# Routing tokens to regions of their two experts in DRAM, in a graph layer with eight experts on one Trainium2 core

## The chip, the cores and the metric

The kernel runs on one core of a Trainium2 chip. The metric is the device time of one execution in microseconds (us). The engines are TensorE (PE, with its weight loads as PEld), VectorE (DVE), ScalarE (ACT), GpSimd (POOL) and SyncE (SP), which here only starts DMAs. Each runs its own list of instructions in order; they meet at semaphores.

## The reference

A graph of 3125 nodes with 256 features and 50000 edges. The layer is a layer norm, two graph convolutions and a linear attention whose results are added to the input, and then a mixture of experts on the normed tokens:

```
xn = layernorm(x)
x = x + gnn(xn, edges) + attention(xn)
tokens = layernorm(x)
probs = softmax(tokens @ router_w.T)            # 8 experts
rw, re = top_k(probs, 2);  rw = rw / rw.sum()
combine = zeros(N, 8).at[arange(N)[:, None], re].set(rw)
out = tokens
for e in range(8):
    h = gelu(tokens @ w1[e] + b1[e])            # 256 -> 256
    out = out + combine[:, e:e+1] * (h @ w2[e] + b2[e])   # 256 -> 256
x = x + out
```

Every token has a weight other than zero for exactly two of the eight experts. All is float32; the kernel makes the expert products from a high and a low float32r part (hi*hi + hi*lo + lo*hi, the table `THREE`), so three matmuls stand for one.

## The kernel before

The 3125 nodes lie in SBUF as 25 slots of 125 partitions; five slots make a chunk (`W` = 5 slots, `C` = 5 chunks, `PT` = 125). The program has these stages:

1. Loads, edge bookkeeping and the projections of the graph and attention weights (0 to 135 us of the trace).
2. The first graph convolution. DVE writes one-hot tiles (`hot_unit`, L584), PE turns 8 of them into counts (`build`, L1009), ACT copies those to SBUF (`take_counts`, L1276), and PE sums with them (`add_sum`, L1092). There are eight blocks of counts (`CH`) of 4 MB, of which three fit in SBUF, so SP stores the first five in DRAM (`kept`, L441) and loads them again (L445). A block may be built over block k only after the store of block k has landed: ACT waits for `kept_ok` (L1283).
3. The second graph convolution (sums from the kept counts, to 510 us). Then, chunk by chunk, PE merges (`merge_transposed`, L1145) and multiplies by the second weights (`times_w2`, L1161), and DVE adds to `acc`, takes mean and variance (L844 to L855) and writes the normed tokens `tok` (L867). PE transposes `tok` (L1170), ACT copies the transposes and splits off the high part (L1385, L1388), DVE the low part (L835), PE makes the router logits (L1179). Meanwhile ACT casts both expert weights to `w_hi` (L1392) and POOL subtracts to make `w_lo` (L484).
4. The router: one pass over all 25 slots on DVE (L878 to L916): top 2, softmax, weights `comb`. Then the second bias is added to `acc` through a small matmul with `comb` (L1202 to L1217, L922).
5. The experts: a hardware loop over five chunks, and inside it all eight experts on all 625 tokens of the chunk. `up` (L1225) makes 24 matmuls of 312 or 314 columns per expert and chunk, ACT applies Gelu with the bias and makes the high part of it (L1428, L1433), DVE the low part (L949), PE makes 30 matmuls of 256 columns (L1251), and DVE adds the result times the token's weight for that expert to `acc` in SBUF (`take`, L930). SP stores each chunk when it is done (L454).

What decides the order is the code of each engine as written and the semaphores; nothing schedules it.

## Time and profile before

| | us |
|---|---|
| median of 3 runs | 905.37 (905.05 to 905.47) |
| the profiled execution | 905.5 |
| its span, first to last instruction | 903.7 |
| stage 5, experts | 614.3 to 899.6 |

In the page, part 1 gives each engine's busy time, part 2 the span in 40 slices of 22.6 us, part 4 the chain of work that ended last. A stage is read from the table of stretches (busy time of each engine in a stretch that one names), and a single hand-over from the instructions in order of time. The granted clock is given as a share of full speed: 1.00 is 2.4 GHz, 0.50 is 1.2 GHz.

### The profile page before, as it was taken

Reading aid. Unit: us, or ns where it says so; the run is one execution under the profiler, and the core shown is the slowest. Engines: PE = TensorE matmul, PEld = TensorE weight load, DVE = VectorE, ACT = ScalarE, POOL = GpSimd, SP = SyncE. Lnnn points to the kernel's source line nnn. Section 1 sums busy time; section 2 is a strip of 40 time slices with the busy share of each in tenths; the row PEclk is TensorE's granted clock in tenths of the full one; section 3 lists DMA queues with packets and bytes.
Section 4 is the critical chain, followed back from the end, with each engine's and each line's share of the span. In section 5 each row is a group of like instructions: output and inputs, shape, how many; then the busy total and the mean of one; then the engine's idle time right before and its main releaser. Section 6 shows DMA issues by size and latency. Waiting matters only on the chain.

```text
span 903.7 us, 16245 instructions
## 1 busy us (share of the span) xinstructions
PE 768.5 (85%) x6482; PEld 700.6 (78%) x6482; DVE 563.4 (62%) x1146; ACT 370.7 (41%) x673; POOL 23.7 (3%) x20
## 2 busy tenths in 40 slices
PE   1697846639999999969999997459999999999997
PEld 0253425539999999749999996448999999999997
DVE  5959986689999995561111188864555455554554
ACT  0036443717777775011111232325434444444442
POOL 1000000000000000000000003300000000000000
PEclk9789786959999999979999998659999999999999
DMA  7200040004444000004862320000000000000000
GB/s 166 51 1 1 1 181 1 1 0 180 183 183 180 7 1 2 1 0 183 339 274 116 112 77 1 1 0 1 1 29 0 0 28 0 28 0 0 28 0 28
DMA packets 10381, 53.98 MB, mean 60 GB/s; under 512 B 1596, under 2 KB 7800, under 8 KB 9050
## 3 DMA queue, kind: packets, MB, share of 16 engines
q1 hardware_dynamic: 10330, 53.25, 16.0%
q8 instruction: 38, 0.62, 0.3%
q14 instruction: 13, 0.11, 0.0%
HBM read 29.57 MB, written 23.68 MB: 59 GB/s over the span
## 4 chain that ended last, share of the span: by engine, by line
PE 68%; DVE 23%; ACT 4%; DMA 2%; issue 1%; SPq 0%; DVEq 0%; POOL 0%; ACTq 0%; POOLq 0%
PE psB L1100 17%; PE psC L1251 8%; PE psD L1251 8%; PE psA L1231 8%; PE psB L1231 8%; PE psC L1100 3%; DVE hot_b L589 3%; PE psA L1017 3%; PE psC L1006 2%; DVE hot_k L589 2%; ACT counts L1285 2%; DMA acc<-in_x_dram 2%; PE psD L1017 2%; PE psD L1157 2%; DVE small L855 1%
## 5 line engine op out<-in xcount | busy, mean ns | idle before, releaser
L1100 PE MATMUL psB<-hs,counts 125*128 125x256 f16 x1600 | 211.4, 276 | 3.4 <-DVE hs L704 2.7
L1100 PEld LDWEIGHTS psB<-hs,counts 125*128 125x128 f16 x1600 | 173.2, 141 | 5.1 <-issue 2.8
L949 DVE TENSOR_TENSOR h_lo<-g_sb,h_hi 128x625 fp32r<-128x625 f32 x80 | 61.2, 807 | 110.0 <-ACT h_hi L1433 110.0
L589 DVE TENSOR_TENSOR hot_b<-iota_j,brow 128x1024 bf16<-128x1024 bf16 x128 | 88.3, 690 | 11.0 <-PE psA L1017 7.6
L1428 ACT ACTIVATE g_sb<-psA,eb 128x312 f32<-128x312 f32 x80 | 37.4, 519 | 129.8 <-PE psA L1231 128.1
L589 DVE TENSOR_TENSOR hot_k<-iota_j,key 128x1000 bf16<-128x1000 bf16 x128 | 86.1, 673 | 0.0
L1017 PE MATMUL psA<-hot_k,hot_b 128*128 128x125 bf16 x512 | 50.9, 224 | 37.0 <-DVE hot_k L589 29.8
L1285 ACT CAST counts<-psA 128x1000 f16<-128x1000 f32 x64 | 63.3, 989 | 38.3 <-PE psA L1017 38.3
L1017 PEld LDWEIGHTS psA<-hot_k,hot_b 128*128 128x128 bf16 x512 | 39.1, 99 | 47.0 <-DVE hot_k L589 35.9
L1285 ACT CAST counts<-psD 128x1000 f16<-128x1000 f32 x64 | 63.6, 993 | 14.3 <-PE psD L1017 14.3
L768 DVE TENSOR_TENSOR sum_both<-psB,sum_both 128x256 f32<-128x256 f32 x32 | 13.5, 422 | 79.7 <-ACT sum_both L1349 79.7
L936 DVE SCALAR_TENSOR_TENSOR acc<-psC,comb,acc 125x256 f32 x100 | 42.7, 476 | 18.7 <-PE psD L1251 18.7
L1006 PE MATMUL psC<-wcat,xnT 128*125 128x512 f32 x100 | 53.4, 662 | 0.8 <-ACT xnT L1270 0.8
L1433 ACT CAST h_hi<-g_sb 128x625 fp32r<-128x625 f32 x80 | 53.1, 719 | 0.0
L1100 PE MATMUL psC<-hs,counts 125*128 125x256 f16 x400 | 52.2, 273 | 0.0
L1017 PE MATMUL psD<-hot_k,hot_b 128*128 128x125 bf16 x512 | 51.0, 224 | 1.0 <-DVE hot_k L589 1.0
L936 DVE SCALAR_TENSOR_TENSOR acc<-psD,comb,acc 125x256 f32 x100 | 42.7, 477 | 13.8 <-PE psC L1251 13.8
L1428 ACT ACTIVATE g_sb<-psB,eb 128x312 f32<-128x312 f32 x80 | 37.4, 520 | 26.6 <-PE psB L1231 26.6
L1017 PEld LDWEIGHTS psD<-hot_k,hot_b 128*128 128x128 bf16 x512 | 40.7, 100 | 8.9 <-DVE hot_k L589 4.6
L1349 ACT COPY sum_both<-psB 128x256 f32<-128x256 f32 x32 | 12.0, 376 | 80.6 <-PE psB L1100 80.6
L1100 PEld LDWEIGHTS psC<-hs,counts 125*128 125x128 f16 x400 | 43.5, 140 | 0.0
L1251 PE MATMUL psC<-w_hi,h_hi 128*125 128x256 f32 x200 | 40.4, 283 | 0.0
(268 smaller groups left out, 1482.5 us busy)
## 6 DMA issues: line engine op xcount, KB each, us to landing
kept_counts<-counts SPq DMA_DIRECT2D x5, 4000.0 KB, 11.8
counts<-kept_counts SPq DMA_DIRECT2D x5, 4000.0 KB, 13.2
w_raw<-in_L_ffn_w_dram SPq DMA_DIRECT2D x2, 2048.0 KB, 12.0
acc<-in_x_dram SPq DMA_DIRECT2D x1, 2800.0 KB
out_dram<-acc SPq DMA_DIRECT2D x5, 560.0 KB
wcat<-in_L_mix_w_qkv_dram SPq DMA_DIRECT2D x1, 384.0 KB
acc<-in_x_dram SPq DMA_DIRECT2D x1, 325.0 KB
out_dram<-acc SPq DMA_DIRECT2D x5, 65.0 KB
```

Of the source, the lines that this page charges most:

```text
L589: v.tensor_tensor(hot[:, slot], iota_j[:, 0:n, :].unsqueeze(1).to_broadcast([P, pairs, n, PAIR]), val[:, cols].rearrange("p (g s) -> p g s ...
L936: y = v.scalar_tensor_tensor(a, out_place(f, d), cw, a, ALU.mult, ALU.add)
L949: v.tensor_tensor(h_lo[:, e % 2, h, :], g_sb[:, h, :], h_hi[:, e % 2, h, :].bitcast(F32), ALU.subtract).then_inc(hidden_low_ok, 1)
L1006: m = pe.matmul(psC[0:PT, 512 * (n % 2):512 * (n % 2) + 512], xnT[:, n % 2, k, :], wcat[:, k, :], start=(k == 0), stop=(k == 1))
L1017: m = pe.matmul(ps[:, bank + KEYS * q:bank + KEYS * q + KEYS], hot_b[:, slot, (GROUP * (j % 2) + q) // PAIR, :, q % PAIR], hot_k[:, slot, ...
L1100: m = pe.matmul(sum_bank(g, d), counts5[0:PT, buf, a, d, :], hs2[0:PT, a, :, :].rearrange("p q f -> p (q f)"), start=a == 0 and first, sto ...
L1157: m = pe.matmul(o, part2[:, part, k, HID * d:HID * d + HID], sel[:, k, PT * c:PT * c + PT], start=False, stop=(k == SECOND_ORDER[-1] and p ...
L1231: m = pe.matmul((psA, psB)[h][:, 512 * n:512 * n + size], (w_hi, w_lo)[a][:, 0, e, k, P * h:P * h + P], (tokT_hi, tokT_lo)[b][:, k, bass.d ...
L1251: m = pe.matmul(out_place(f, d), (h_hi, h_lo)[a][:, f % 2, k, PT * d:PT * d + PT], (w_hi, w_lo)[b][:, 1, f, k, :], start=(i == 0 and k == ...
L1285: act.copy(counts[:, k % BUFFERS, UNIT * u:UNIT * u + UNIT, :].rearrange("p (h s) j -> p h (s j)", h=2), (psA, psD)[unit % 2][:, :].rearra ...
L1428: g = act.activation(g_sb[:, h, at + had:at + size], (psA, psB)[h][:, 512 * n + had:512 * n + size], ACT.Gelu, bias=eb1[:, 2 * e + h:2 * e ...
L1433: act.copy(h_hi[:, e % 2, h, :], g_sb[:, h, :]).then_inc(hidden_high_ok, 1)
```

## The change

All eight experts on all tokens become two experts per token.

- **Regions.** A DRAM tensor `slots` has a region of 3328 rows (`REGION`) for each expert and 256 spare rows. A row is 265 floats (`ROW`, 1060 bytes): the token, its eight weights and its node number. After the inputs have landed, SP fills all of it with zeros, in pieces of 130 floats: 28.5 MB, ahead of the kept counts in SP's queue.
- **Router by chunk.** The pass of stage 4 becomes `router(c)`, in five parts between the chunks of stage 3. PE computes each token's place in its expert's region from sums of one-hot rows (`ranks`), DVE makes it an address (`slot_places`), and POOL scatters the chunk's 125-row slots: 10 indirect DMAs a chunk (5 slots, 2 experts each), 50 in all. The tiles `rows` are double-buffered; before DVE writes the tokens of chunk c it waits for the scatters of chunk c-2.
- **Output.** `x + tokens` of a chunk goes to `out` at once (SP waits for `tok_added`).
- **Tiles.** `MOE_TILES` is 32: tiles of 256 rows of one expert, the worst case; a table made by DVE (`tab_e`, `tab_r`) says for each which expert and where. For each tile SP loads the rows (`xs`, four buffers) and copies the expert's first weights from SBUF to SBUF (`w1_now`, two buffers, two copies of 2 KB per partition); PE transposes the rows (4 transposes), makes `up` (12 matmuls of 256 columns) and `down` (14, with the second bias as one of 7 for each half); ACT and DVE split and apply Gelu as before, on 512 columns; DVE multiplies by the weight into `y` (three buffers); POOL adds `y` to `out` by two indirect DMAs that accumulate. POOL waits until all adds of the tile before have landed (`added`). Rows that are all zero get node number 4095 and are left out by the bounds check. SP, ACT, DVE and PE each read the expert's number from SBUF into a register (`value_load`), SP the place too.
- **Weights' low part.** `w_lo` moves from POOL to DVE, behind the last `slot_places`.
- **One-hot tiles.** The two DVE instructions of `hot_unit` (1024 and 1000 elements) become one of 2048.

```diff
+            sp.wait_ge(zeros_ok, 1)
+            sp.wait_ge(in_x, 32)
+            for e in range(EXPERTS + 1):
+                size = REGION if e < EXPERTS else SLOT
+                run = 130 if e < EXPERTS else 106
...
             for k in range(SPILLED):
                 sp.wait_ge(counts_ok, UNITS * (k + 1))
...
+            sp.wait_ge(table_ok, 2)
+            sp.wait_ge(spread, 16 * 2 * SLOTS)
+            sp.wait_ge(w_lo_ok, 2)
+            for t in range(-2, MOE_TILES):
+                if t + 2 < MOE_TILES:
+                    n = t + 2
+                    at = sp.value_load(tab_r[0:1, n:n + 1], min_val=0, max_val=EXPERTS * REGION)
...
+                    sp.dma_start(xs[:, n % X_BUFS], slots[bass.ds(at, SLOT), :].rearrange("(p q) f -> p q f", q=2)).then_inc(slots_in[n % X_BUFS], 16)
+                if t >= 0:
+                    e = sp.value_load(tab_e[0:1, t:t + 1], min_val=0, max_val=EXPERTS - 1)
+                    if t >= 2:
+                        sp.wait_ge(upped, 2 * t - 2)
+                    for part, w in enumerate((w_hi, w_lo)):
+                        sp.dma_start(w1_now[:, t % 2, part].bitcast(F32), w[:, 0, bass.ds(e, 1), :, :].rearrange("p a k f -> p (a k) f").bitcast(F32)).then_inc(w1_now_in[t % 2], 16)
...
-                pool.tensor_tensor(w_lo[:, i], w_raw[:, i], w_hi[:, i].bitcast(F32), ALU.subtract).then_inc(w_lo_ok, 1)
...
+            for c in range(C):
+                pool.wait_ge(weights_in_row, c + 1)
+                pool.wait_ge(place_ok, c + 1)
+                for d in range(W):
+                    for j in range(2):
+                        n = W * c + d
+                        pool.indirect_dma_start(slots[:, :], bass.IndirectOffsetOnAxis(place[0:PT, j, n:n + 1], 0), rows[0:PT, c % 2, d, :],
+                                                None).then_inc(spread, 16)
+            pool.wait_ge(stored, 32 * C)
+            for t in range(MOE_TILES):
+                if t:
+                    pool.wait_ge(added, 16 * 2 * t)
+                for q in range(2):
+                    pool.wait_ge(y_ok, 2 * t + q + 1)
...
+                    pool.indirect_dma_start(out[:, :], bass.IndirectOffsetOnAxis(to_row[:, t % 3, q:q + 1], 0), y[:, t % 3, q, :], None,
+                                            bounds_check=NODES - 1, oob_is_err=False, compute_op=ALU.add).then_inc(added, 16)
...
+                if c >= 2:
+                    slot_places(c - 2)
                 v.wait_ge(std_ok, c + 3)
                 st.did(v.reciprocal(rstd[0:PT, 0:W], small[0:PT, 3, 0:W]))
                 st.wait()
...
+                if c >= 2:
+                    v.wait_ge(spread, 16 * 2 * W * (c - 1))
```

In order, the places that matter. DVE in chunk 2, before: statistics, the addition of the chunk before, then the tokens.

```order
L850 BN_STATS stats<-acc 125x6 x4
L853 BN_AGGR mv<-stats 125x2 [waits vector_done]
L853 BN_AGGR mv<-stats 125x2 x4
L855 TENSOR_SCALAR small<-mv 125x5 [waits vector_done]
L859 TENSOR_TENSOR acc<-acc,tok 125x1280 [waits tok_ok]
L861 RECIPROCAL rstd<-small 125x5 [waits std_ok]
L867 TENSOR_SCALAR tok<-acc,mv,rstd 125x256 [waits tok_transposed,tok_added,vector_done]
L867 TENSOR_SCALAR tok<-acc,mv,rstd 125x256 x4
```

The same place in the change (`rows` holds the tokens, `spread` counts landed scatters):

```order
L986 TENSOR_SCALAR small<-mv 125x5 [waits vector_done]
L958 TENSOR_TENSOR place_of<-psC,region_at 125x40 [waits rank_in]
L960 TENSOR_REDUCE members<-member 125x8
L962 TENSOR_TENSOR passed<-passed,members 125x8 [waits vector_done]
L963 TENSOR_TENSOR picked<-pick,place_of 125x80
L965 TENSOR_REDUCE place_f<-picked 125x10 [waits vector_done]
L967 CAST place<-place_f 125x2x5 [waits vector_done]
L990 RECIPROCAL rstd<-small 125x5 [waits std_ok]
L995 TENSOR_SCALAR rows<-acc,mv,rstd 125x256 [waits spread,vector_done]
L995 TENSOR_SCALAR rows<-acc,mv,rstd 125x256 x4
```

The places of chunk 0 are made here, and two instructions on DVE waits for the scatters that use them.

POOL in the change, at the last scatters and the first two tiles; before, POOL had only the two `w_lo` subtractions and a memset in this part of the program.

```order
L565 DMA expert_slots<-rows,place 26880x265 [waits place_ok,weights_in_row]
L565 DMA expert_slots<-rows,place 26880x265 x9
L574 DMA out_dram<-y,to_row 3125x256 [waits gate_row_ok,y_ok,stored]
L574 DMA out_dram<-y,to_row 3125x256 [waits gate_row_ok,y_ok]
L574 DMA out_dram<-y,to_row 3125x256 [waits gate_row_ok,y_ok,added]
L574 DMA out_dram<-y,to_row 3125x256 [waits gate_row_ok,y_ok]
```

Each tile's two adds now stand in a row, and the first of them waits for the landing of the two before.

PE in the change, `down` of one tile (`psC` and `psD` take one half each), with the read of the expert's number ahead of it; before, this was a row of 30 matmuls per expert and chunk without such a read.

```order
L1344 TENSOR_LOAD tab_e
L1344 ISA x2
L1377 ISA [waits y_ok,hidden_low_ok]
L1377 MATMUL psC<-b_both,b_ones 128x256
L1380 ISA
L1380 MATMUL psC<-w_hi,h_hi 128x256
L1380 ISA
L1380 MATMUL psC<-w_hi,h_hi 128x256
```

The two ISA lines and the load set up registers; `down` moved behind them, once for each of 32 tiles.

## Rows read from the trace of the kernel before

**Rows 1.** The page, part 1: busy time in us (share of the span), instructions
```profile
PE 768.5 (85%) x6482; PEld 700.6 (78%) x6482; DVE 563.4 (62%) x1146; ACT 370.7 (41%) x673; POOL 23.7 (3%) x20
```
**Rows 2.** Stretches: us, each engine's busy us (instructions), PEclk, DMA share, GB/s
```profile
215.00:350.00 135.00, 129.28 (x1508) 124.57 (x1507) 128.99 (x227) 103.16 (x131) 0.00 (x0) 1.00 0.29 123
...
510.00:614.00 104.00, 70.58 (x708) 65.65 (x706) 76.70 (x221) 32.73 (x50) 19.74 (x3) 0.79 0.13 41
614.00:904.00 290.00, 283.00 (x2160) 282.09 (x2160) 143.26 (x280) 123.27 (x240) 0.00 (x0) 0.99 0.04 11
```
**Rows 3.** The chain that ended last, 664 to 690 us: start, us, what
```profile
679.38 3.00 PE psC L1251 x24
...
683.08 1.74 PE psA L1231 x12
```
**Rows 4.** Groups of instructions, 614 to 904 us: shapes and count, busy us, mean ns, idle before
```profile
L949 DVE TENSOR_TENSOR h_lo<-g_sb,h_hi 128x625 fp32r<-128x625 f32 x80 | 61.2, 807 | 110.0 <-ACT h_hi L1433 110.0
L1433 ACT CAST h_hi<-g_sb 128x625 fp32r<-128x625 f32 x80 | 53.1, 719 | 0.0
L936 DVE SCALAR_TENSOR_TENSOR acc<-psD,comb,acc 125x256 f32 x100 | 42.7, 477 | 13.8 <-PE psC L1251 13.8
...
L1428 ACT ACTIVATE g_sb<-psB,eb 128x312 f32<-128x312 f32 x80 | 37.4, 520 | 26.6 <-PE psB L1231 26.6
```
**Rows 5.** DVE in order of time, chunks 2 and 4: start, us, instruction, idle before
```profile
538.13 1.65 DVE L844 SCALAR_TENSOR_TENSOR acc<-psB,second_scale,acc 125x256 f32<-125x256 f32 x4
...
542.46 6.71 DVE L855 TENSOR_SCALAR small<-mv 125x5 f32<-125x5 f32 x1
...
550.70 1.70 DVE L867 TENSOR_SCALAR tok<-acc,mv,rstd 125x256 f32<-125x256 f32 x5
552.56 1.46 DVE L835 TENSOR_TENSOR tokT_lo<-tokT,tokT_hi 128x1250 fp32r<-128x1250 f32 x1 [0.16 <-ACT tokT_hi L1388]
...
571.01 6.69 DVE L855 TENSOR_SCALAR small<-mv 125x5 f32<-125x5 f32 x1
```
**Rows 6.** POOL in order of time, the first subtraction for `w_lo`
```profile
540.31 8.83 POOL L484 TENSOR_TENSOR w_lo<-w_raw,w_hi 128x4096 fp32r<-128x4096 f32 x1 [535.74 <-ACT w_hi L1392]
```
**Rows 7.** PE in order of time, transposes of five slots of tokens
```profile
532.86 1.02 PE L1174 MATMUL psA<-ident,tok 125*128 125x125 f32 x8
```
**Rows 8.** The chain that ended last, 560 to 616 us: the router and the second bias
```profile
591.57 0.38 DVE logit L879
...
593.80 3.49 DVE topi L885 x26
...
602.71 1.90 PE psA L1208 x8
...
608.91 4.96 DVE acc L922 x5
```
**Rows 9.** SP's DMA issues in order of time: start, us, what
```profile
17.30 3.56 SPq L436 DMA_DIRECT2D gpre<-in_L_mix_g_pre_dram  x2
...
123.78 161.03 SPq L441 DMA_DIRECT2D kept_counts<-counts  x5
...
899.64 0.76 SPq L454 DMA_DIRECT2D out_dram<-acc  x2
```
**Rows 10.** SP's waits at the end, 890 to 904 us: us in total, times, longest
```profile
SPq L93 <- DMA out_dram<-acc: 2.9, 1, 2.9
```
**Rows 11.** Stretches: DMA rates with 4-byte to 1 KB pieces, then with 1 KB pieces
```profile
20.00:24.00 4.00, 4.00 (x10) 0.75 (x8) 0.00 (x0) 0.00 (x0) 0.00 (x0) 1.00 1.00 124
...
515.00:523.00 8.00, 7.17 (x100) 6.63 (x98) 3.05 (x9) 2.03 (x3) 0.00 (x0) 1.00 1.10 352
```
**Rows 12.** Stretches around clock changes: PE busy, and PEclk third from the end
```profile
114.00:117.00 3.00, 2.27 (x12) 0.96 (x9) 3.00 (x5) 2.48 (x6) 0.00 (x0) 1.00 0.00 0
...
612.00:615.00 3.00, 1.16 (x7) 0.87 (x6) 1.86 (x3) 0.71 (x1) 0.00 (x0) 1.00 0.00 0
615.00:618.00 3.00, 3.00 (x15) 3.00 (x14) 0.00 (x0) 0.89 (x2) 0.00 (x0) 0.56 0.03 5
```

More of the change, by code:

```diff
@@ L839, in _ @@
                 a = acc[0:PT, W * c:W * c + W, :]
+                tok = rows[0:PT, c % 2]
                 if c == 0:
@@ L940, in _ @@
[L940 to L951 removed]
+            v.tensor_scalar(tab_r[:], tile_at_r[:], float(EXPERTS * REGION), None, ALU.min).then_inc(table_ok, 1)
@@ new lines, in _ @@
+                        m.then_inc(upped, 1)
+                if t >= 0:
+                    e = expert_of(t)
+                    pe.wait_ge(hidden_low_ok, t + 1)
+                    if t >= 2:
+                        pe.wait_ge(y_ok, 2 * t - 2)
+                    for q in range(2):
+                        o = (psC, psD)[q][:, 512 * (t % 2):512 * (t % 2) + DIM]
+                        pe.matmul(o, b2_ones[:, :], b2_both[:, bass.ds(e, 1), :].rearrange("p a f -> p (a f)"), start=True, stop=False)
+                        for i, (a, b) in enumerate(THREE):
+                            for k in range(2):
+                                m = pe.matmul(o, (h_hi, h_lo)[a][:, t % 2, k, P * q:P * q + P],
+                                              (w_hi, w_lo)[b][:, 1, bass.ds(e, 1), k, :].rearrange("p a f -> p (a f)"), start=False, stop=(i == 2 and k == 1))
@@ L1411, in _ @@
[L1411 to L1416 removed]
+                if c >= 1:
+                    odds_exp(c - 1)
+            token_copies(C - 1)
+            odds_exp(C - 1)
+            act.wait_ge(merged, 2 * C)
@@ L1417, in _ @@
+            weights_high(0)
             act.preload_act_table(ACT.Gelu)
             act.wait_ge(router_ok, 2)
-            with act.Fori(0, C) as c:
-                base = EXPERTS * c
-                for e in range(EXPERTS):
-                    act.wait_ge(down, base + (e + 1))
-                    for h in range(2):
-                        act.wait_ge(upped, 2 * base + (2 * e + h + 1))
-                        act.wait_ge(hidden_low_ok, 2 * base + (2 * e + h + 3))
-                        for n, (at, size, had) in enumerate(HALVES):
-                            g = act.activation(g_sb[:, h, at + had:at + size], (psA, psB)[h][:, 512 * n + had:512 * n + size], ACT.Gelu,
-                                               bias=eb1[:, 2 * e + h:2 * e + h + 1])
-                        g.then_inc(hidden_ok, 1)
-                    for h in range(2):
-                        act.wait_ge(hidden_ok, 2 * base + (2 * e + h + 5))
-                        act.copy(h_hi[:, e % 2, h, :], g_sb[:, h, :]).then_inc(hidden_high_ok, 1)
+            act.wait_ge(table_ok, 2)
@@ new lines, in _ @@
+            for t in range(-2, MOE_TILES):
+                if t + 2 < MOE_TILES:
+                    n = t + 2
+                    act.wait_ge(slots_transposed, n + 1)
+                    if n >= 2:
+                        act.wait_ge(upped, 2 * n - 2)
+                    act.copy(xT_hi[:, n % 2], psA[:, 512 * (n % 2):512 * (n % 2) + 512].rearrange("p (k s) -> p k s", k=2)).then_inc(slots_high_ok, 1)
+                if 0 <= t + 1 < MOE_TILES:
+                    n = t + 1
+                    e = act.value_load(tab_e[0:1, n:n + 1], min_val=0, max_val=EXPERTS - 1)
+                    sa.did(act.copy(bias_now[:, n % 2, :], eb1[:, bass.ds(2 * e, 2)]))
+                    sa.wait()
+                    if n >= 2:
+                        act.wait_ge(hidden_low_ok, n - 1)
+                        act.wait_ge(down, 2 * n - 2)
+                    for h in range(2):
+                        act.wait_ge(upped, 2 * n + h + 1)
+                        act.activation(g_sb[:, n % 2, h, :], psB[:, 512 * h:512 * h + SLOT], ACT.Gelu,
+                                       bias=bias_now[:, n % 2, h:h + 1]).then_inc(hidden_ok, 1)
+                    act.wait_ge(hidden_ok, 2 * n + 2)
+                    act.copy(h_hi[:, n % 2], g_sb[:, n % 2]).then_inc(hidden_high_ok, 1)
```

518 lines of the change are left out of this document (292 added, 226 removed).

## The prediction

> **What bounds the kernel now.** I read the page first [rows 1]: PE is busy 85% of the span, POOL 3%. Then the table of stretches [rows 2]: the experts, 614 to 904 us, are the longest stage, and PE is busy 283.0 of 290 us there at clock 0.99, while DVE has 143.3 and ACT 123.3. So this stage is PE's. The chain inside it [rows 3] shows one expert on one chunk: 24 matmuls of 256 columns in 2.85 us (0.119 us each, so 30 take 3.56) and 2 x 1.74 us for the 24 of 312 columns. That is 7.04 us, and 40 of them are 282 us of the 285.3 us from 614.3 to 899.6. The stage ahead of it, 510 to 614, has PE at 70.6 of 104 us: no engine fills it, it is a chain of hand-overs, and this is where the change puts new ones.
>
> **The experts on PE.** New work per tile of 256 rows: `up` 12 x 0.119 = 1.43 us, `down` 14 x 0.119 = 1.67 us, four transposes at 1.02/8 = 0.13 us each or less [rows 7], 0.45 us. That is 3.55 us a tile, 32 tiles 114 us in place of 282. If only PE counted, 168 us would be won. The tiles are 32 whatever the routing, so none of this depends on the data.
>
> **The experts on ACT and DVE.** ACT per tile: 512 columns out of PSUM about 0.6, two Gelus of 256 about 0.46 each (312 take 0.52 [rows 4]), the high part of 512 about 0.62 (625 take 0.72), a bias copy 0.2: 2.3 us. DVE: two low parts of 512 at 0.69 each (0.81 for 625), two results at 0.41, two small ones at 0.17: 2.5 us. Each of PE, ACT, DVE also reads a register from SBUF once a tile, and no row shows that; below 0.3 us it would vanish, at the 2.9 us that SP waits for its last store to land [rows 10] it would bound the loop at some 5.4 us. Part of it lies beside queued work; I take 1 us, so the engines could turn a tile in about 4.0 us.
>
> **The experts on POOL.** This is what I expect to bound. The adds of tile t wait until those of t-1 have landed, so a tile costs POOL two issues and one landing: P = 2g + L, with g the time POOL spends on one indirect DMA of 125 to 128 rows. L: SP's wait after the last store, 2.9 us [rows 10], for 625 KB, while a tile adds 256 KB but also reads what it adds to; I take 2.9 (2.4 to 4). g is in no row. The nearest: an issue by SP of one plain store, 0.76/2 = 0.38 us, and of one with 128 pieces of 4 bytes, 3.56/2 = 1.78 us [rows 9]. A list of 128 addresses is nearer to the latter, and POOL works in software on its own scale; I take 1.3. Then P = 5.5 us and the loop 32 x 5.5 = 176 us; at the ends 4.0 (engines) and 6.5.
>
> The trace has a landing of 2.9 us [rows 10]. The Trainium skill, "DMA: Bandwidth & Descriptors", section on the anatomy of a DMA from GpSimd, gives a fixed 2.0 us for one such DMA, most of it the receipt of the write, and calls the making of descriptors small; by that a tile would cost POOL about 3 us and the loop would be the engines'. That is rival A.
>
> DMA volume per tile: rows 0.27 MB, weights 0.52 MB, adds 0.26 MB twice: 1.3 MB, 3.8 us at the 352 GB/s of 1 KB pieces [rows 11]. It fits under 5.5, and hardly under 4.0.
>
> **The chunks, 510 to 614.** Chunks 0 and 1 should end about 541, when the router of chunk 0 has had its logits from PE (before, chunk 1 ended at 538.1 [rows 5]). From chunk 2 on one turn of DVE is: additions, statistics and variance 4.3 us (538.13 to 542.46 [rows 5]); `slot_places` six small steps, 1.5; the wait for the scatters; tokens 1.7 and the addition 1.5 (as for the 1250 elements of L835); the router, of which the old pass took 591.6 to 602.7 for 25 slots [rows 8], a fifth of the 5.3 us of top and index (591.95 to 597.29) and ten steps of 0.2, 3.2. That is 12.4 us and the wait. The wait is the point: the places of chunk c-2 are released just before, and DVE then waits until its ten scatters have landed: 10g + L = 15.9 us (6.7 to 20.7), with only PE's next merge beside it. Three turns are 3 x 28.3 = 85 us, to 626. Then `slot_places(3)`, to 627.5, and 20 more scatters and a landing, 28.9 us: 656.4. DVE's own tail lies under this: the last router and places to about 634, the biases' parts 4, both `w_lo` at 4.4 us each (1250 elements 1.46, 625 elements 0.81, so 1.04 ns each), the table 2.6: 649. It takes over once g is below about 0.9.
>
> What goes: DVE stood at L855, an instruction of 0.17 us elsewhere, for 6.71 us, from 542.46 to 549.17, while POOL's subtraction ran from 540.31 to 549.14 [rows 5, 6]; a second time at 571.01. So 13.1 us of the old stage was DVE held by POOL. The old router pass and the second bias (591.6 to 614.3 [rows 8]) go too. What stands in the turns above already leaves them out.
>
> The Trainium skill, "SBUF — State Buffer", section on the two separate sides, says that a DMA started from GpSimd needs the same port for its descriptors, and that a DVE instruction in a fast mode keeps it out until it ends. Rows 5 and 6 agree that one of the two holds the other, the other way round. By this rule g would be longer in the loop than between the chunks, where DVE waits; no row prices that, and it is a reason for the upper ends.
>
> **Start of the loop.** First rows loaded (2.9), the first weights behind them, transposes, splits, `up`, Gelu, `down`: 13 us, so the adds start at 669.4. With the loop, 845.4; the span ends there plus 0.3, and with the 1.8 us that the profiled execution had around its span (905.5 against 903.7) the time is 847.5. The median is 0.1 below the profiled execution. **Forecast 848 us.** By differences: 285.3 to 176 in the loop wins 109, the start moves from 614.3 to 669.4 and costs 55, the old end (stores, 3.8 us) goes.
>
> **The zeros.** 28.5 MB from about 29 us on, beside nothing on the DMAs. The first kept store is behind them in the queue and must land by about 238 us, when ACT starts block 3 (the five issues end at 284.8 [rows 9], and are 22.7 us apart). So the fill has 197 us if 12 are left for the store: 145 GB/s are needed. Pieces of 520 bytes lie between 352 GB/s (1 KB pieces) and 124 GB/s (mostly 4 bytes to 1 KB) [rows 11]; nearer the first, say 220. Cost nothing; if it were 124, see B.
>
> **One-hot tiles.** One DVE instruction of 2048 for two of 2024 elements saves one start in each of 128 units. In 215 to 350 us PE is busy 129.3 of 135 us [rows 2], so DVE is not what ends there; I count 0, and up to 2 us in either direction (PE now waits for both halves at once).
>
> **Rivals.**
> A, scatters are cheap and the engines bound the loop. For it: L of one small DMA may be below 2.9. Against: three of four engines also wait for registers. With g = 0.5, waits of 7.9: `slot_places(3)` at 603.5, DVE's tail ends 625, adds from 638, 32 x 4.0 = 128: 766.3 and 2.1 is 768 us. Chance 0.17.
> B, the zeros are slow. At 124 GB/s they end at 259, the first kept block lands at 271 in place of 238, and the first convolution waits 32 us: 880. Chance 0.10.
> C, the clock. At 114 to 117 us PE was busy 76% and had 1.00; at 612 to 615 it was busy 39% and the next 3 us had 0.56 [rows 12]. The loop would have PE busy 3.55 of 5.5, 65%, between these. At 1.2 GHz a tile takes PE 7.1 us, more than 5.5, so it would be busy again and the clock come back; if it stayed at 0.50, 32 x 1.6 = 51 us more: 899. Chance 0.10.
> D, slower than before: scatters are dear. Each 0.1 us of g costs 3.0 (three waits) + 2.0 (last twenty) + 6.4 (loop) = 11.4 us. The 57 us of gain are gone at g = 1.8. For it: SP's 1.78 us for 128 pieces, an accumulate that reads first, the port. With g = 2.2 the time is 848 + 103 = 951. Chance 0.18.
> Forecast, g from 1.0 to 1.6: 814 to 882, chance 0.45.
>
> **How the numbers follow.** Faster is the forecast, A, B and nearly all of C: 0.81. Slower is D and a little of C: 0.17; 0.02 within 0.2%, about what a measurement of this kernel can tell from none. For 8 in 10 the range goes from 780, leaving out the cheap half of A, to 915, leaving out the dear two thirds of D.
>
> **What would show it.** The loop: POOL's two DMAs and a landing of about 5.5 us a tile, SP, PE and DVE waiting for `added` in the end. Three waits of DVE at L995 of about 16 us. L986 at 0.17 us throughout. DMA at about 28 MB before 160 us and no wait of ACT for the first kept block. PE at 1.00 in the loop. I am wrong most likely in g or L, which appear 114 and 35 times in the sum; or in the register reads, if a tile takes more than POOL's chain.

## The result and the profile after the change

| | before | after |
|---|---|---|
| median | 905.42 us (905.05 to 909.44, 4 runs) | 916.04 us (912.74 to 919.88, 4 runs) |
| profiled execution, its span | 905.5, 903.7 | 912.74, 910.9 |

The changed kernel is slower by 1.0%: ratio 1.0102, 95% interval 1.0082 to 1.0123. The forecast was 848 us, and the result lies just above the range of 780 to 915.

The page, parts 1 and 2, of the kernel after. It answers to [rows 1]: PE fell from 768.5 to 649.5 us, and POOL rose from 23.7 to 173.2.

```profile
PE 649.5 (71%) x5262; PEld 560.1 (61%) x5262; DVE 494.0 (54%) x1008; ACT 320.4 (35%) x591; POOL 173.2 (19%) x134
...
PEclk9789786969999999989999996755558888888796
```

PE is busy for 119 us less, and the profiled execution takes 7.2 us more (the median 10.6). The stretches from the chunks on, after (columns as in [rows 2]): 545 to 676 is the router and the scatters, 700 to 900 the loop over the tiles.

```profile
545.00:676.00 131.00, 38.20 (x251) 34.02 (x247) 48.84 (x197) 17.81 (x27) 67.56 (x50) 0.56 0.24 66
700.00:900.00 200.00, 152.22 (x885) 130.52 (x883) 75.47 (x179) 67.35 (x144) 92.12 (x60) 0.86 0.60 141
```

No engine fills either stretch. In the first, POOL leads with 67.6 of 131 us. In the loop PE is busy 76% at a clock of 0.86, where [rows 2] had 98% at 0.99.

What one indirect DMA costs POOL: POOL in order of time, after, between the chunks (L565, scatters of 125 rows of 1060 bytes) and then in the loop (L574, adds of 128 rows of 1 KB).

```profile
632.25 1.19 POOL L565 DMA_INDIRECT expert_slots<-rows,place  x1 [11.09 <-DVE place L967]
633.74 1.19 POOL L565 DMA_INDIRECT expert_slots<-rows,place  x1 [0.30 <-issue]
...
750.74 1.55 POOL L574 DMA_INDIRECT out_dram<-y,to_row  x1 [3.97 <-DMA out_dram<-y,to_row]
752.60 1.54 POOL L574 DMA_INDIRECT out_dram<-y,to_row  x1 [0.30 <-issue]
757.12 1.55 POOL L574 DMA_INDIRECT out_dram<-y,to_row  x1 [2.98 <-DMA out_dram<-y,to_row]
758.98 1.54 POOL L574 DMA_INDIRECT out_dram<-y,to_row  x1 [0.30 <-issue]
```

A scatter is 1.19 us busy and 0.30 of issue: 1.49 us from start to start. An add is 1.85. These are the g of the prediction, which had 1.3 for both. From the end of the second add to the first of the next tile POOL waits 2.98 or 3.97 us for the landing here. From 692.76, the first add, to 903.04, the first of the last tile, 31 tiles pass: 6.78 us a tile.

**Where the time went**, by the steps of the prediction and the trace after:

| step | predicted | measured | difference |
|---|---|---|---|
| `slot_places(3)` done | 627.5 | 631.3 | +3.8 |
| all scatters landed | 656.4 | 676.2 | +16.0 more |
| first add | 669.4 | 692.8 | +3.6 more |
| loop ended | 845.4 | 910.6 | +41.8 more |

The sum is 65.2 us, the whole distance from 847.5 to 912.7. The second and the last rows carry it.

### The profile page after: what moved, and what is told of

Its sections match the earlier page's. It is cut to its first block, busy times and chain, and to the rows that moved or that the text cites. A ratio compares the mean times of both kernels' runs of the same rounds, so it can differ in the third digit from the quotient of the medians.

```text
span 910.9 us, 14119 instructions
## 1 busy us (share of the span) xinstructions
PE 649.5 (71%) x5262; PEld 560.1 (61%) x5262; DVE 494.0 (54%) x1008; ACT 320.4 (35%) x591; POOL 173.2 (19%) x134
## 4 chain that ended last, share of the span: by engine, by line
PE 46%; DVE 23%; DMA 10%; POOL 7%; issue 5%; ACT 4%; SPq 3%; DVEq 0%; POOLq 0%; ACTq 0%
PE psB L1212 17%; POOL expert_slots L565 7%; DMA w_now<-w_lo 6%; DVE hot L677 6%; PE psB L1367 5%; PE psC L1118 3%; PE psC L1212 3%; PE psA L1130 3%; PE psC L1380 2%; PE psD L1380 2%; PE psD L1130 2%; DMA acc<-in_x_dram 2%; DMA expert_slots<-rows,place 2%; PE psD L1268 1%; DVE qkv L726 1%
## 5 line engine op out<-in xcount | busy, mean ns | idle before, releaser
L677 DVE TENSOR_TENSOR hot<-iota_j,places 128x2048 bf16<-128x2048 bf16 x128 | 155.2, 1223 | 15.6 <-PE psA L1130 9.9
L574 POOL DMA_INDIRECT out_dram<-y,to_row x64 | 99.5, 1555 | 133.5 <-DMA out_dram<-y,to_row 60.3
L1367 PE MATMUL psB<-xT_hi,w_now 128*128 128x256 f32 x256 | 60.5, 348 | 44.7 <-DMA w_now<-w_lo 44.7
L565 POOL DMA_INDIRECT expert_slots<-rows,place x50 | 67.6, 1351 | 94.6 <-issue 52.4
L1367 PEld LDWEIGHTS psB<-xT_hi,w_now 128*128 128x128 f32 x256 | 47.8, 243 | 48.6 <-DMA w_now<-w_lo 48.6
L1130 PE MATMUL psA<-hot 128*128 128x125 bf16 x512 | 50.6, 224 | 36.9 <-DVE hot L677 34.0
L1130 PEld LDWEIGHTS psA<-hot 128*128 128x128 bf16 x512 | 39.0, 100 | 47.1 <-DVE hot L677 36.2
L1558 ACT ACTIVATE g_sb<-psB,bias_now 128x256 f32<-128x256 f32 x64 | 30.2, 474 | 64.9 <-PE psB L1367 53.6
L1130 PE MATMUL psD<-hot 128*128 128x125 bf16 x512 | 50.2, 222 | 1.1 <-DVE hot L677 1.1
L1130 PEld LDWEIGHTS psD<-hot 128*128 128x128 bf16 x512 | 40.1, 99 | 8.5 <-DVE hot L677 3.7
```

Of the source, the lines that this page charges most:

```text
L565: pool.indirect_dma_start(slots[:, :], bass.IndirectOffsetOnAxis(place[0:PT, j, n:n + 1], 0), rows[0:PT, c % 2, d, :], None).then_inc(spre ...
L574: pool.indirect_dma_start(out[:, :], bass.IndirectOffsetOnAxis(to_row[:, t % 3, q:q + 1], 0), y[:, t % 3, q, :], None, bounds_check=NODES ...
L677: v.tensor_tensor(hot[:, slot].rearrange("p g w n s -> p (g w) n s"), iota_j[:, :, :].unsqueeze(1).to_broadcast([P, 2 * pairs, P, PAIR]), ...
L1130: m = pe.matmul(ps[:, bank + KEYS * q:bank + KEYS * q + KEYS], hot[:, slot, pair, 0, :, s], hot[:, slot, pair, 1, 0:KEYS, s], start=True, ...
L1367: m = pe.matmul(psB[:, at:at + SLOT], w1_now[:, n % 2, a, k, P * h:P * h + P], (xT_hi, xT_lo)[b][:, n % 2, k, :], start=(i == 0 and k == 0 ...
L1558: act.activation(g_sb[:, n % 2, h, :], psB[:, 512 * h:512 * h + SLOT], ACT.Gelu, bias=bias_now[:, n % 2, h:h + 1]).then_inc(hidden_ok, 1)
```

## Experiments

In all of them a tile's pitch is the distance from its first DMA to that of the next, a mean over the 31 distances of one profiled loop (two profiles of the changed kernel have 6.78 and 6.90; the last three distances are short, for a reason given in the last section). The columns of the order of time are start, duration, instruction and, in brackets, the idle time before it and what ended it.

### What made twenty scatters take 44 us

The last twenty scatters of the changed kernel are not all alike. DVE and POOL in order of time, after:

```profile
639.94 1.21 DVE L1005 CAST b_both<-b_raw 64x2048 fp32r<-64x2048 f32 x1
641.19 2.28 DVE L1007 TENSOR_TENSOR b_both<-b_raw,b_both 32x2048 fp32r<-32x2048 f32 x1
643.50 8.76 DVE L1011 TENSOR_TENSOR w_lo<-w_raw,w_hi 128x4096 fp32r<-128x4096 f32 x2
```

```profile
639.71 1.79 POOL L565 DMA_INDIRECT expert_slots<-rows,place  x1 [0.30 <-issue]
641.81 2.73 POOL L565 DMA_INDIRECT expert_slots<-rows,place  x1 [0.31 <-issue]
644.84 4.14 POOL L565 DMA_INDIRECT expert_slots<-rows,place  x1 [0.30 <-issue]
649.29 4.03 POOL L565 DMA_INDIRECT expert_slots<-rows,place  x1 [0.30 <-issue]
657.26 1.20 POOL L565 DMA_INDIRECT expert_slots<-rows,place  x1 [3.94 <-issue]
```

Four scatters are long. The last three of them end 1.1 us after an instruction of DVE ends (643.47 and 644.54, 647.88 and 648.98, 652.26 and 653.32; the two subtractions of `w_lo` are one line of two instructions of 4.38 us), as if they had begun only there. The first, which began ahead of the cast, ends 0.35 us after it. The four cost 7.9 us more than four others. A gap of 3.94 us follows, ahead of the fortieth scatter. Theory: DVE holds them. Rival: they are slow by themselves, for a queue that is full or DMAs that lag.

**e2: DVE's large work after the scatters.**

```diff
+            v.wait_ge(spread, 16 * 2 * SLOTS)
             v.wait_ge(in_b2, 32)
             st.did(v.tensor_copy(b2_both...
```

> DVE computes b2_both, w_lo and the tables only once all fifty scatters have landed, so no DVE work of any size lies beside the last twenty scatters. If DVE's work was what stretched them: all fifty at 1.19 busy and 1.49 from start to start, the twenty take 29.8 and the last lands at about 665 (changed kernel: 676.2), then b2_both, w_lo and the tables follow with 16 us, rows are loaded from 681 on (changed kernel 676), time 921. If they were slow by themselves (a full queue, DMAs that lag): landing again at 676, rows loaded from 692, time 932.

Measured: 920.91 us (919.55 to 924.47), ratio to before 1.0174 (1.0148 to 1.0200); DVE's theory had 921, its rival 932. POOL in order of time, e2:

```profile
637.66 1.19 POOL L565 DMA_INDIRECT expert_slots<-rows,place  x1 [0.30 <-issue]
639.15 1.19 POOL L565 DMA_INDIRECT expert_slots<-rows,place  x1 [0.30 <-issue]
640.65 1.18 POOL L565 DMA_INDIRECT expert_slots<-rows,place  x1 [0.31 <-issue]
642.14 1.19 POOL L565 DMA_INDIRECT expert_slots<-rows,place  x1 [0.30 <-issue]
646.93 1.20 POOL L565 DMA_INDIRECT expert_slots<-rows,place  x1 [3.60 <-issue]
```

All twenty take 1.18 to 1.20, so DVE's instructions made the four long. The gap ahead of the fortieth scatter is still there, 3.60 us with no instruction of another engine beside it. It is ahead of the fortieth scatter in the profile of every kernel here that has two buffers for the rows (ten profiles), and in none of the three with four (e1, e8, e9). Its cause stays open.

The Trainium skill, "SBUF — State Buffer", section on the two separate sides, says that GpSimd cannot write descriptors while a DVE instruction holds the port that they share. This trace agrees for the cast: 1.79 us, against 1.19 in e2. For a DVE instruction with two inputs in SBUF the same section has the port held only against a GpSimd instruction that reads SBUF. Here the subtractions with both operands in SBUF made scatters take 2.73, 4.14 and 4.03 us; whether such a DMA counts as reading SBUF no run here shows. The prediction cited the page as a reason for the upper ends and put no price on it. The price was 7.9 us, and it fell on the last scatters, where the prediction had laid DVE's tail "under" them at no cost.

**e1: four buffers for the rows.** Chunk c waits for the scatters of chunk c-4 in place of c-2. The rows of the tiles, `xs`, move into the dead `hs` for space.

```diff
-            rows = sb("rows", [P, 2, W, ROW], F32, st)
+            rows = sb("rows", [P, 4, W, ROW], F32, st)
...
-                if c >= 2:
-                    v.wait_ge(spread, 16 * 2 * W * (c - 1))
+                if c >= 4:
+                    v.wait_ge(spread[c - 4], 16 * 2 * W)
```

> The buffer of rows that the scatters read has four parts in place of two (the loaded rows of the experts' loop, xs, lie in the dead hs to make room), so DVE's waits for scatters in chunks 2 and 3 go and that of chunk 4 waits for chunk 0 alone; 55.3 us of waits in the changed kernel. Rule of the last twenty scatters (DVE's work holds POOL's descriptor writing back): the scatters start at 546 as before, but DVE now works beside all of them, and some of them take 1.8 to 4.1 us in place of 1.19; the last lands between 635 and 665 us (changed kernel: 676), time 875 to 905, 888 my estimate. Rival (the slow scatters had another cause): 50 x 1.49 = 75 us from 546, last landing at 624, time 864. Rival two, the waits were hidden by something else: 916.

Measured: **869.55 us** (867.34 to 873.21), ratio to before 0.9608 (0.9578 to 0.9638): faster than both kernels, by this alone. It lies between my two cases, 888 (875 to 905) with the hold by DVE and 864 without it, and below the range of the first: the hold is there, but I had it too dear. DVE's three waits at L995 are gone. In the changed kernel they were, by the table of waits between 510 and 640 us (engine, line, what it waited for, us in total, times, longest):

```profile
DVE rows L995 <- DMA expert_slots<-rows,place: 55.3, 3, 18.8
```

In e1 no such row is left, and the fifty scatters run in one row from 546.11 to 629.66. POOL in order of time, e1, beside the same DVE work, which now comes at 587.7 to 600.2:

```profile
588.39 1.79 POOL L566 DMA_INDIRECT expert_slots<-rows,place  x1 [0.30 <-issue]
590.48 2.02 POOL L566 DMA_INDIRECT expert_slots<-rows,place  x1 [0.30 <-issue]
592.80 4.15 POOL L566 DMA_INDIRECT expert_slots<-rows,place  x1 [0.30 <-issue]
597.25 4.03 POOL L566 DMA_INDIRECT expert_slots<-rows,place  x1 [0.30 <-issue]
```

The hold moves with DVE's work, 7.2 us here. Two further scatters, beside the addition of the tokens (L999, 1.49 us, both operands in SBUF), took 1.75 and 2.25 and ended 1.1 us after it. All of it together is 9 us. The adds start at 650.5 in place of 692.8. The prediction's time of DVE's wait, 15.9 us, was near the 18.4 measured. But it was treated as a given cost of the change, and it is only the cost of having two buffers: 10 scatters are 15 us, and DVE's own turn is 11.9 (593.87 to 623.97 from one L995 to the next, less the wait of 18.23).

### What sets a tile's 6.78 us

Three things can: POOL's ring (two adds and a landing, 2g + L), a ring over SP, and the engines.

The second ring is seen in SP's order and PE's waits. For tile t, SP first issues the rows of tile t+2, for which it waits for the gate of tile t-2. Only then it issues the copy of expert weights of tile t from `w_hi` and `w_lo` to `w1_now`. PE needs that copy for `up`. SP's waits in the changed kernel (line, what it waited for, us in total, times, longest; L521 is the wait for the gate):

```profile
SPq L521 <- DVE gate L1053: 82.1, 26, 8.9
```

PE in order of time, after, then the stretches around it (columns as in [rows 2]):

```profile
750.56 0.80 PE L1367 MATMUL psB<-xT_hi,w_now 128*128 128x256 f32 x2 [4.22 <-DMA w_now<-w_lo]
```

```profile
747.00:748.00 1.00, 0.00 (x0) 0.00 (x0) 0.94 (x3) 0.19 (x1) 0.00 (x0) 1.00 0.96 296
748.00:749.00 1.00, 0.00 (x0) 0.00 (x0) 0.00 (x0) 0.00 (x0) 0.00 (x0) 1.00 0.78 234
749.00:750.00 1.00, 0.00 (x0) 0.00 (x0) 0.00 (x0) 0.00 (x0) 0.00 (x0) 0.71 0.88 264
750.00:751.00 1.00, 0.44 (x2) 0.44 (x3) 0.00 (x0) 0.00 (x0) 0.26 (x1) 0.50 0.55 210
...
758.00:759.00 1.00, 1.00 (x7) 1.00 (x6) 0.18 (x1) 0.45 (x1) 0.69 (x2) 0.50 0.00 0
759.00:760.00 1.00, 1.00 (x8) 1.00 (x8) 0.69 (x1) 0.42 (x3) 1.00 (x1) 0.67 0.83 80
```

PE stands for 4.22 us, the granted clock falls to 0.50 (1.2 GHz) as it stands, and it stays there while PE is busy again, until 759. In that stretch a pair of matmuls of 256 columns is recorded with 0.63 us in place of 0.40. So here a late copy costs PE twice, and it can reach POOL as a late `y`.

**e3: half of the adds.**

```diff
-                for q in range(2):
+                for q in range(1):
```

> Only the first of a tile's two DMAs to the output is issued; the rows of the other half of each tile are left out of the result. POOL's ring is then g + L = 1.85 + 3.1 = 5.0 us a tile in place of 6.8. If POOL's ring alone bounds the loop: 32 x 5.0 = 158, time 858. If the ring over SP, the copied weights and the gate (10.6 to 12.6 us for two tiles in the trace) is right behind it: 5.3 to 6.3 a tile, loop 170 to 200, time 868 to 898, my estimate 884.

Measured: 884.15 us (878.5 to 885.43), ratio 0.9745 (0.9707 to 0.9782); the pitch is 5.93 us. POOL hardly waits for landings now. Waits from 690 us on, e3:

```profile
POOL out_dram L574 <- DVE y L1062: 149.8, 30, 19.5
...
POOL out_dram L574 <- DMA out_dram<-y,to_row: 5.4, 2, 3.5
```

So POOL's ring bounds the changed kernel, and the next limit is only 0.85 us below it, not at the 4.0 that the prediction gave to the engines.

**e4: the copies ahead of the rows in SP's order.** In the loop of SP the block `if t >= 0` (copies of tile t) stands ahead of `if t + 2 < MOE_TILES` (rows of tile t+2).

> SP issues a tile's copy of the expert's weights ahead of the rows of two tiles later, so the copy no longer stands behind SP's wait for the gate of tile t-2. PE's waits for w1_now (44.7 us in 16) should go. If the two rings disturb each other (mean 6.78 us, shortest 6.35): the loop falls towards 32 x 6.35 = 203, time 902 to 910. If POOL's ring bounds alone: 916, no change.

Measured: 910.04 us (905.71 to 912.25, 10 runs), ratio 1.0033 (1.0013 to 1.0052). The profiled loop has a pitch of 6.85 us, no better than 6.78, and PE waits for the copies as before, 36.5 us in 21 times. The profiled run is at its second stage 2.4 us earlier than the changed kernel, and that stage is not touched by this edit: `w_raw` is issued at 506.85 us against 509.20, while the twelve profiles of kernels that are alike up to there reach it between 506.85 and 509.57. So a part of the 6 us is no effect of the edit, and the profile shows none in the loop. What remains of it is not settled, and the 902 to 910 of my first case did not come from the loop.

**e5: no copies at all** after tile 1 (w1 is left out).

```diff
-                if t >= 0:
+                if 0 <= t < 2:
                     e = sp.value_load(...)
...
-                    pe.wait_ge(w1_now_in[n % 2], 32 * (n // 2 + 1))
+                    pe.wait_ge(w1_now_in[n % 2], 32)
```

> The copies of the first weights (2 x 256 KB a tile from w_hi and w_lo to w1_now) are made for tiles 0 and 1 alone, so all later tiles are computed with the wrong expert's first weights: the computation of w1 is left out. It tells what sets the tile's 6.78 us, where half of the adds gave 5.93 and weights issued earlier gave 6.85. Theory: POOL's ring, with its landing stretched by the copies' traffic in the same 16 DMA engines (150 GB/s in the loop): two adds 1.85 + 1.55 and a landing of 2.95 (as between the chunks, where nothing else is on the DMAs) give 6.35, loop 32 x 6.35 = 203, 902 us. Rival (the landing of an adding DMA is 3.3 us by itself): pitch stays at 6.8, 916 us. PE's 44.7 us of waits for w_now go in either case.

**e11: the same copies, to a place that nobody reads.**

```diff
-                        sp.dma_start(w1_now[:, t % 2, part].bitcast(F32), ...).then_inc(w1_now_in[t % 2], 16)
+                        to = w1_now[:, t % 2, part].bitcast(F32) if t < 2 else spare[:, t % 3, part]
+                        sp.dma_start(to, ...).then_inc(w1_now_in[t % 2] if t < 2 else copy_in[t % 3], 16)
```

(Not shown: from tile 5 on SP also waits for the copy of three tiles before.)

> The copies of the first weights are made as in the changed kernel, the same bytes at the same place in SP's order, but from tile 2 on into the dead hs, and PE computes with the weights of tiles 0 and 1 and waits for no copy: w1 is left out as in e5. It takes e5's gain (6.78 to 6.40 us a tile) apart. If the copies' traffic in the DMAs stretches the landing of the adds: 6.8 a tile, 913 to 916 us. If it is PE's waits for the copies, after which its clock is 0.50 for some 10 us (749 to 759 us in the changed kernel) and the tile comes late to POOL: 6.4 a tile as in e5, 901 us.

> The changed kernel once more beside it, unchanged, for the comparison with the run above: 916 us, 6.8 us a tile.

Measured: e5 901.01 us (892.37 to 901.29 in three executions, and 1332.04 in a fourth, which the ratio leaves out; its cause is not known), ratio 0.9889 (0.9829 to 0.9950), pitch 6.40; e11 911.23 us (908.13 to 912.04), ratio 1.0054 (1.0033 to 1.0075), pitch 6.70; the changed kernel beside e11 916.65 us (910.02 to 920.76), pitch 6.90. POOL in order of time, e5 and then e11:

```profile
753.00 1.55 POOL L574 DMA_INDIRECT out_dram<-y,to_row  x1 [2.97 <-DVE to_row L1052]
754.86 1.54 POOL L574 DMA_INDIRECT out_dram<-y,to_row  x1 [0.30 <-issue]
759.43 1.55 POOL L574 DMA_INDIRECT out_dram<-y,to_row  x1 [3.02 <-DVE to_row L1052]
```

```profile
749.44 1.55 POOL L581 DMA_INDIRECT out_dram<-y,to_row  x1 [3.11 <-DVE to_row L1059]
751.30 1.54 POOL L581 DMA_INDIRECT out_dram<-y,to_row  x1 [0.30 <-issue]
757.01 1.55 POOL L581 DMA_INDIRECT out_dram<-y,to_row  x1 [4.17 <-DVE to_row L1059]
```

(The releaser is put down to `to_row`, which DVE writes for a tile two ahead once the same landing has come; it is the landing that POOL waits for.) Without the copies the wait is 2.9 to 3.0 us in most tiles, and these take 6.4. With the copies' traffic it is up to 4.3, though PE waits for none of them. So of the changed kernel's 6.8 to 6.9 us a tile, 6.4 are two adds and a landing beside no copies, and 0.3 is traffic of the copies that stretches the landing (6.70 against 6.40). The 0.1 to 0.2 that are left for PE's waits are no more than the 0.12 between two profiles of the changed kernel, so that share is not shown. I had expected one of the two to be all of it.

The clock is no effect of the waits for weights alone. A stretch of the loop of the changed kernel, then of e11, where PE waits for no copy:

```profile
700.00:860.00 160.00, 122.65 (x714) 105.18 (x713) 60.54 (x143) 55.93 (x120) 72.58 (x47) 0.87 0.65 152
```

```profile
700.00:860.00 160.00, 126.93 (x745) 110.66 (x745) 57.30 (x148) 56.62 (x125) 73.10 (x47) 0.85 0.64 155
```

In e11 PE stands for other things, since POOL sets the pace, and its clock is as low.

### What if the ring over POOL is opened

**e6 and e7: plain writes to a scratch.** The outputs of a token's first choice go to rows 0 to 3124 of a scratch in DRAM and those of the second to the next 3125. No row is written twice, and nothing is added in the DMA. In e6 each tile still waits for the landing of the one before; in e7 it doesn't. After the loop the scratch is loaded, and DVE adds it to `acc`.

```diff
-                    pool.indirect_dma_start(out[:, :], ..., y[:, t % 3, q, :], None,
-                                            bounds_check=NODES - 1, oob_is_err=False, compute_op=ALU.add).then_inc(added, 16)
+                    pool.indirect_dma_start(parts[:, :], ..., y[:, t % 3, q, :], None,
+                                            bounds_check=2 * NODES - 1, oob_is_err=False).then_inc(added[t % 3], 16)
...
+            for c in range(C):
+                for j in range(2):
+                    sp.dma_start(part_at(j, c), parts[NODES * j:NODES * j + NODES, :]...[:, c]).then_inc(parts_in[c], 16)
```

> The experts' outputs are written plainly (no add in the DMA) to a scratch in DRAM, the first choice of a token in its first 3125 rows and the second in the next; each tile still waits for the landing of the tile before. After the loop the scratch is loaded, DVE adds it to acc and SP stores the output once, some 28 us by my estimate (6.4 MB in and 3.2 MB out at 352 GB/s); the stores of the chunk stage go. If adding is what makes a DMA 1.85 us from start to start where the scatters have 1.49: pitch 1.49 again and a tile 5.7 to 6.1, 32 x 5.9 = 189, time 915. If it is something else (128 rows, the bound on the rows): 1.85 and 6.8 a tile as before, time 944.

> As the run before, but no tile waits for the landing of another: rows of the scratch are written once each, so only the reuse of y after three tiles is waited for. POOL needs 3.0 to 3.7 us a tile. If the ring over SP, the weights and the gate is what half of the adds met (5.93): 32 x 5.9 = 189, time 915. If it was still POOL's landing that held it: PE's 4.0 a tile plus what the copies cost, 32 x 4.5 = 144, time 870.

Measured: e6 947.94 us (941.67 to 951.76), pitch 6.09; e7 939.09 us (935.17 to 943.94), pitch 5.86. Both are slower than the changed kernel, and their loops are faster, by 22 and 29 us. POOL in order of time, e6:

```profile
760.86 0.97 POOL L585 DMA_INDIRECT expert_outputs<-y,to_row  x1 [3.60 <-DMA expert_outputs<-y,to_row]
762.14 0.97 POOL L585 DMA_INDIRECT expert_outputs<-y,to_row  x1 [0.30 <-issue]
```

128 plain rows cost POOL 0.97 + 0.30 us where 128 added rows cost 1.55 + 0.30. Adding in the DMA costs POOL 0.58 us more for each, 1.2 us a tile. And e7 without any wait on a landing turns a tile no faster than e3: the limit at 5.9 is the ring over SP (e8 shows it), with PE waiting 32.5 us in 19 times for `w1_now` in e7.

The times miss my expectations, 915 for both, by the end and not by the loop: from the last write of e7 at 873.65 to the end of its span at 934.8 are 61 us, where I had 28.

**e8: e7, with the buffers of e1 and the order of e4.**

> The run before with four parts of the rows' buffer (46 us faster by itself) and SP's weights ahead of the rows. Sum if both rings over POOL and SP are cut: start of the adds 650.5, 32 x 4.8 = 154, end of the loop 804, merge of the scratch 28, time 834. If SP's order is worth nothing here too: 32 x 5.9, time 869.

Measured: **844.66 us** (843.24 to 845.88), ratio 0.9316 (0.9295 to 0.9336). I had 834: the loop was quicker (4.21 us a tile in place of 4.8), and the end took 60 us in place of 28. A stretch of e8:

```profile
655.00:780.00 125.00, 123.88 (x863) 108.05 (x862) 78.02 (x205) 65.11 (x140) 57.24 (x60) 1.00 0.65 220
```

PE is busy 99% of the loop at a clock of 1.00. SP's order was worth nothing while POOL's ring bound (e4), and opening POOL's ring won 0.9 us a tile while SP's order bound (e7). Together they won 2.6. The buffers of the rows are no part of that: by themselves they leave the pitch at 6.7 (e1). The prediction gave 4.0 us a tile to the engines; 4.2 were measured, and they can be had only with both rings open. That the two are near is luck in part. The 4.0 were 3.55 of PE's work and an allowance for reading the expert's number from SBUF. In e8 PE is busy for all of the 4.2 at clock 1.00: `down` takes 2.35 us from its first matmul at 705.82 to the next transposes at 708.17, where I had 14 x 0.119 = 1.67.

**e9: the loads of the scratch in two parts.** Stretches of e8 and then of e9, while the scratch is loaded (in e9 with the first stores of the output in it):

```profile
786.00:812.00 26.00, 0.00 (x0) 0.00 (x0) 5.97 (x4) 0.00 (x0) 0.00 (x0) 0.50 0.32 133
```

```profile
786.00:812.00 26.00, 0.00 (x0) 0.00 (x0) 14.82 (x10) 0.00 (x0) 0.00 (x0) 0.50 1.01 293
```

```diff
-                    sp.dma_start(part_at(j, c), ...[:, c]).then_inc(parts_in[c], 16)
+                    for lo, hi in ((0, 112), (112, PT)):
+                        sp.dma_start(part_at(j, c)[lo:hi], ...[lo:hi, c]).then_inc(parts_in[c], 16)
```

> The run e8_free_four_buffers with each load of the scratch in two parts, 112 and 13 rows, as the stores of out are, in place of one of 125 rows. In e8 the loads moved at 133 GB/s with the DMAs busy by a third, and 61 us lay between the last write of the loop and the end. If the shape is what held them: 6.4 MB at 330 GB/s in 19 us, then one chunk's adds (3.0) and the last stores, tail 30 to 35 us, time 815 to 820. If reading DRAM just written is slow by itself: no change, 844.

Measured: **817.74 us** (815.99 to 819.75), ratio to before 0.9021 (0.9001 to 0.9041). It is the fastest version, 9.8% under the kernel before. From the last write to the end of the span are 36 us now (780.4 to 816.8). A load of 125 rows had 0.32 of the DMAs and 133 GB/s; 112 rows and 13 rows have all of them and 293. The Trainium skill, "DMA: Bandwidth & Descriptors", section on why a DMA increments its semaphore by 16, says that the number of DMA engines is the largest up to 16 that divides the sizes of the slowest dimension. For 125 rows that is 5 of 16, 0.31, and the trace agrees with 0.32.

### The one-hot tiles

**e10: two DVE instructions of 1024 elements for the one of 2048.**

```diff
-                val = places[:, column // PAIR:column // PAIR + pairs].rearrange("p g w s -> p (g w) s")
-                v.tensor_tensor(hot[:, slot]..., ALU.is_equal).then_inc(hot_ready, 1)
+                for which in range(2):
+                    val = places[:, column // PAIR:column // PAIR + pairs, which, :]
+                    v.tensor_tensor(hot[:, slot, :, which], ..., ALU.is_equal).then_inc(hot_ready, 1)
...
-                    pe.wait_ge(hot_ready, g // 2 + 1)
+                    pe.wait_ge(hot_ready, g + 2)
```

> The changed kernel with the one-hot tiles of a unit made by two DVE instructions of 1024 elements again, in place of one of 2048; the rest of the change stays. By the trace of the changed kernel its second stage starts 1.65 us earlier than before the change, which I ascribe to this edit: 917.7 us, 0.2% above the changed kernel. If the shift came from elsewhere: 916.

Measured: 920.00 us (915.09 to 923.13, 6 runs), ratio 1.0144 (1.0116 to 1.0172), against 1.0102 (1.0082 to 1.0123) for the changed kernel: 4 us, with intervals that overlap, and the second measurement of the changed kernel (1.0118, 1.0056 to 1.0180) overlaps more. In its profile w_raw is issued at 512.07 us, outside the 506.85 to 509.57 of all twelve profiles with the single instruction, and 2.9 later than in the changed kernel. So this part of the change may be worth some 3 us, where I had 0 with bounds of 2. One profile and these intervals do not show it, nor do they decide between the 917.7 and the 916 that I expected.

## Why the prediction was wrong

**The mechanism was right, its size was not.** Under "The experts on POOL" it says "This is what I expect to bound", and it did (e3, and the 60.3 us in which POOL waits for landings in the loop). P = 2g + L was the right formula, and g was the term that was mis-sized. I took 1.3 us between SP's 0.38 and 1.78 [rows 9]; the adds have 1.85 and the scatters 1.49. I chose below the row of 1.78 us that I had called the nearest one, and took one g for two kinds of DMA, though the rival named "an accumulate that reads first". What the add costs is 0.58 us for each DMA (e6).

By the prediction's own derivatives: scatters 0.19 over in 5.0 us per 0.1 are 9.5 us, and adds 0.55 over for the first and 0.25 for the second (whose issue gap lies in the landing) give 0.8 us a tile, 26 us. That is 35 of the 65.

**Terms at zero that were not zero**, 30 us:
- DVE's tail under the last scatters: 7.9 us of hold (e2), from a rule that I had cited and not priced. The gap ahead of the fortieth scatter: 3.6 us, open.
- L in the loop: 2.9 was right without the copies (e5: mostly 2.93 to 3.02), but the DMA volume was only checked for fitting in, not for what it does to a landing. Traffic, and late weights if they cost anything: 0.4 us a tile, 12 us.
- The start of the loop: 16.6 us from the last landing to the first add, where I had 13. The rest of some 3 us lies in hand-overs at the chunks and the end.

The rule of the shared port was put in the wrong place: g was to be longer in the loop by it. There DVE's instructions take 0.7 us and less, and of 64 adds 63 took 1.54 to 1.62 us and one 1.90; the hold came ahead of the loop, at the last scatters.

Two slips in the prediction's sums changed little: the parts of DVE's turn add up to 12.2 us and not 12.4, and [rows 3] shows 3.00 us for 24 matmuls and not 2.85, which other pieces of that chain have.

**The missing step** was SP's queue. I priced engines and POOL, and never followed what SP's next DMA waits for. The copy of tile t behind the gate of tile t-2 made a ring of 5.9 us (e3, e7). Rival A, 768 us with cheap scatters and engines that bound at 4.0, could therefore not happen in this kernel: with POOL free it still had 5.9. Its 0.17 were wrongly placed.

**The rivals.** D, slower because indirect DMAs are dear, is what happened, but not by its mechanism alone: with the measured g the sum gives 848 + 35 = 883, still faster than before, and the 30 us of terms at zero carry it over. I let each rival stand by itself and never added a half-dear g to a few small losses. 0.17 was too little for the slow side. B, slow zeros: the fill ran at 160 GB/s and not 220, until 203.5 us, and not "before 160". It needed 145, so its cost was 0 as forecast. SP's issues, after:

```profile
24.81 178.68 SPq L490 DMA_DIRECT2D expert_slots<-zeros  x9
203.54 81.22 SPq L494 DMA_DIRECT2D kept_counts<-counts  x5
```

C, the clock: it fell in part, 0.86 over the loop, where "PE at 1.00 in the loop" was to be seen. It is as low in e11, where PE waits for no weights, and 1.00 in e8, where PE is busy throughout. Its price is not shown: POOL's ring sets the pace, and at most 0.2 us a tile lie between e11 and the changed kernel.

**What was right:** the waits at L995 (15.9 forecast, 18.4 measured, three of them); L855's 6.71 us gone, now 0.17 at L986 as said, twice 6.5 us won; the start of the scatters, 546.8 by the terms of the sum and 545.98 measured. `slot_places(3)` came within 3.8 us, but by luck: the three waits were 7.6 us longer than forecast and all the rest 3.8 shorter.

**Why the good versions are good.** The change turned 282 us of PE's work into 134 (32 x 4.2 in e8), and paid for it with three rings through DMAs: DVE's on two row buffers (55 us), POOL's on its own landings, SP's on a gate. e1, e7 and e4 open one each. Only e1 pays alone.

## What to carry to other kernels

Where a change replaces an engine's work by DMAs that wait for one another, write down every ring with its queue, also that of the engine which only issues, and take the second longest beside the longest: it bounds what mending the first can bring (6.78 to 5.9 here, and 4.2 with both). A wait that the change adds is a choice of the number of buffers before it is a cost. And work laid "under" a run of GpSimd DMAs is not free when it is DVE's and its instructions are long (1.2 to 4.4 us here).

## What the runs showed of the hardware that was not expected

- Indirect DMAs cost GpSimd time by kind, all with 0.30 us of issue behind: 0.97 us for 128 plain rows of 1 KB, 1.19 for 125 rows of 1060 bytes, 1.55 for 128 added rows. The Trainium skill, "DMA: Bandwidth & Descriptors", section on the anatomy of a DMA from GpSimd, calls the making of descriptors small. Here POOL is busy for half a landing with each (1.55 us against 2.9 to 3.0); for what a DMA costs POOL the measurement decides. How much of it is the making of descriptors no run here shows.
- The landing of added DMAs, from the end of the second on POOL, took 2.9 to 3.0 us in most tiles without the copies (e5) and up to 4.3 beside 0.5 MB of copies a tile (e11), but for the first tiles, with up to 4.8 in both.
- In the last tiles the wait is 1.94, 2.68 and 1.94 us after the change, and the distances are 5.33, 6.08 and 5.33. From 889 to 906 us the DMAs move 0 GB/s beside these adds, from which I infer that the bounds check leaves all their rows out. They still cost POOL 1.55 and 0.30 us each. Without these three distances a tile takes 6.91 us in place of 6.78.
- The granted clock was 1.00 until 749 us and 0.50 from 750 to 759, though PE was busy again from 750.6. It had stood for 4.2 us before.
- Writes of 520-byte pieces from SBUF to DRAM ran at 160 GB/s beside little else.
- The same code reached its second stage between 506.85 and 509.57 us in twelve profiles; differences of 2 us between single profiles there say nothing.
